# Four cross-attention layers on one core: the softmax of the narrow layers read straight from PSUM

## The reference

```
narrow (layers 0, 3):  xn = x / sqrt(mean(x^2) + 1e-5) * norm_w
                       q = xn Wq (16 heads of 8);  k, v = ctx Wk, ctx Wv (4 heads of 8, each for 4 query heads)
                       x = x + softmax(q k^T / sqrt(8)) v Wo
wide (layers 1, 2):    q = x Wq; k, v = ctx Wk, ctx Wv (16 heads of 64)
                       x = x + softmax(q k^T / 8 + col_bias) v Wo + bo
```

## Time and profile before

| | |
|---|---|
| median of 3 runs | 418.3 us (417.02 to 418.61) |
| profiled execution, its own time | 416.49 us |
| its span | 414.7 us |
| mean granted clock of TensorE | 0.978 |
| share of the span busy: PE, DVE, ACT, POOL | 91%, 68%, 64%, 47% |
| exponentials (L432) | 512 of 389 ns |
| narrow, wide maxima (L545) | 256 of 343 ns, 256 of 283 ns |

### The profile page before, as it was taken

One profiled execution on the slowest core, in us unless ns is written; L12 is line 12 of the kernel. 1 busy time (PEld: TensorE's weight loads), 2 busy tenths in 40 slices (PEclk: granted clock), 3 DMA queues, 4 the chain that ended last, 5 costly groups with the idle time before them and its releaser, 6 DMA issues.

```text
span 414.7 us, 10513 instructions
## 1 busy us (share of the span) xinstructions
PE 377.7 (91%) x3536; PEld 326.8 (79%) x3536; DVE 279.9 (68%) x1439; ACT 265.7 (64%) x1143; POOL 194.4 (47%) x222
## 2 busy tenths in 40 slices
PE   5686989999999999988997999999999999987865
PEld 4565877898899998877875878889999988866644
DVE  5578468564647656578475777758775575688993
ACT  4456567775657565567474777769865765666680
POOL 5845534332324233466472776424433333667751
PEclk9696989999999999999999999999999999999999
DMA  8705100000000000000000000000000000000000
GB/s 267 303 3 213 42 0 3 2 2 0 4 0 2 2 2 2 1 2 2 2 7 9 8 3 6 2 2 2 2 2 2 2 2 1 2 2 2 8 9 13
DMA packets 4740, 9.72 MB, mean 23 GB/s; under 512 B 592, under 2 KB 3152, under 8 KB 4432
## 3 DMA queue, kind: packets, MB, share of 16 engines
q1 hardware_dynamic: 4400, 8.72, 5.7%
q10 hardware_dynamic: 288, 0.33, 0.3%
HBM read 8.53 MB, written 0.52 MB: 22 GB/s over the span
## 4 chain that ended last, share of the span: by engine, by line
PE 75%; DVE 17%; ACT 3%; issue 2%; DMA 1%; POOL 1%; ACTq 0%; DVEq 0%; POOLq 0%
PE pt_ps L757 12%; PE scores_ps L744 8%; DVE probs L545 8%; PE v_ps L806 8%; PE fill_ps L629 7%; PE q_ps L711 7%; PE fill_ps L630 7%; PE fill_ps L631 7%; PE v_ps L776 6%; PE v_ps L788 6%; PE scores_ps L731 5%; DVE probsT L556 4%; ACT probs L432 2%; DVE oT L563 1%; DMA tok_i<-in_tokens 1%
## 5 line engine op out<-in xcount | busy, mean ns | idle before, releaser
L432 ACT ACTIVATE probs<-probs,negmax 128x128 f32<-128x128 f32 x512 | 198.4, 389 | 120.1 <-DVE negmax L545 120.1
L342 POOL TENSOR_TENSOR probs<-probs,inv 128x512 f32<-128x512 f32 x128 | 133.1, 1040 | 204.5 <-DVE inv L552 203.1
L432 ACT ACTIVATION_READ_ACCUMULATOR probs<-probs,negmax 128x1 f32 x512 | 95.6, 187 | 0.0
L545 DVE CUSTOM_DVE_ANT_0 probs<-scores_ps,col_bias,inv_rms 128x128 f32<-128x128 f32 x256 | 73.4, 343 | 22.7 <-PE scores_ps L731 22.3
L556 DVE COPY probsT<-pt_ps 128x512 f32<-128x512 f32 x128 | 82.1, 682 | 4.2 <-PE pt_ps L757 2.1
L545 DVE CUSTOM_DVE_ANT_0 probs<-scores_ps,col_bias 128x128 f32<-128x128 f32 x256 | 58.2, 283 | 37.8 <-PE scores_ps L744 37.8
L757 PE MATMUL pt_ps<-smalls,probs 128*128 128x128 f32 x512 | 71.7, 284 | 0.0
L757 PEld LDWEIGHTS pt_ps<-smalls,probs 128*128 128x128 f32 x512 | 56.3, 144 | 12.2 <-issue 10.9
L629 PE MATMUL fill_ps<-c_hi,w_hi 128*128 128x256 f32 x128 | 39.1, 305 | 4.6 <-DVE kn_lo L516 4.6
L545 DVE DVE_READ_ACCUMULATOR2_ANT negmax<- 128x1 f32 x512 | 42.4, 83 | 0.0
L776 PE MATMUL v_ps<-probsT,v_narrow 128*32 128x128 f32 x512 | 35.0, 280 | 6.9 <-issue 3.3
(11 more groups left out here) (87 smaller groups left out, 567.5 us busy)
## 6 DMA issues: line engine op xcount, KB each, us to landing
kT<-in_kv_w SPq DMA_DIRECT2D x6, 512.0 KB, 6.7
w_qo<-in_qo_w SPq DMA_DIRECT2D x2, 1024.0 KB, 9.6
v<-in_ctxT SPq DMA_DIRECT2D x4, 256.0 KB, 3.9
v<-in_kv_w SPq DMA_DIRECT2D x2, 512.0 KB, 11.1
outT<-x SPq DMA_DIRECT2D x8, 64.0 KB, 1.6
x<-in_xT SPq DMA_DIRECT2D x1, 384.0 KB, 7.9
oT<-in_narrow_kv ACTq DMA_DIRECT2D x1, 320.0 KB, 3.0
wn<-in_narrow_w SPq DMA_DIRECT2D x2, 128.0 KB, 4.8
```

Source lines behind the costliest of these rows:

```text
L342: nc.gpsimd.tensor_tensor(p4, p4, inv[:, o % 2, side, :].unsqueeze(2).broadcast_to([P, 4, S]), ALU.mult,).then_inc(probs_made[side], 1)
L432: last = nc.scalar.activation(e, e, ACT.Exp, scale=-1.0, bias=negmax[:, o % 2, side, q:q + 1], accum_out=rowsum[:, o % 2, side, q:q + 1])
L545: last = nc.vector.tensor_tensor_reduce(out=probs[:, o % PROBS_RING, side, cols], in0=scores_ps[side][:, cols], in1=bias, scale=scale, sca ...
```

## The change

In narrow octets, each side's four custom instructions give way to one tensor_reduce (maximum over keys, 512 columns of PSUM into 4) and a tensor_scalar that multiplies these four by inv_rms and -1. A semaphore most_made stands between the two. The exponentials of narrow octets read the scores in PSUM, with inv_rms as the scale and negmax as the bias, and write probs. The queries are no longer negated. The wait for rms_made moves from ahead of the scores' wait to behind the first reduction. The scores of the next octet wait, where the octet before in the same bank was narrow, for exps_made of both sides instead of scores_read. Octets from LAST_FILL + 2 = 55 on that are odd count as using the fill_ps banks: narrow ones (57, 59, 61, 63) write there. Octet 55 is wide and still writes scores_ps, and waits for the fill banks' reads. The third plane of col_bias and its memset go.

```diff
@@ exponentials
+                n = o // 2
                 act.wait_ge(scores_read[side], o + 1)
                 for q in range(4):
-                    e = probs[:, o % PROBS_RING, side, q * S:(q + 1) * S]
-                    last = nc.scalar.activation(e, e, ACT.Exp, scale=-1.0, bias=negmax[:, o % 2, side, q:q + 1],
+                    cols = slice(q * S, (q + 1) * S)
+                    e = probs[:, o % PROBS_RING, side, cols]
+                    if is_narrow(n):
+                        scores, scale = banks[scores_bank(o)][side][:, cols], inv_rms[:, n % 2:n % 2 + 1]
+                    else:
+                        scores, scale = e, -1.0
+                    last = nc.scalar.activation(e, scores, ACT.Exp, scale=scale, bias=negmax[:, o % 2, side, q:q + 1],
                                                 accum_out=rowsum[:, o % 2, side, q:q + 1])
@@ scores_out
-                if l in NARROW and h == 0 and side == 0:
-                    dve.wait_ge(rms_made, narrow_index(n) + 1)
                 dve.wait_ge(scores_full[side], o + 1)
+                if l in NARROW:
+                    use = 2 * narrow_index(n) + h + 1
+                    nc.vector.tensor_reduce(most[:, side, :], banks[scores_bank(o)][side][:].rearrange("p (h k) -> p h k", h=4),
+                                            mybir.AxisListType.X, ALU.max).then_inc(most_made[side], 1)
+                    if h == 0 and side == 0:
+                        dve.wait_ge(rms_made, narrow_index(n) + 1)
+                    dve.wait_ge(most_made[side], use)
+                    nc.vector.tensor_scalar(negmax[:, o % 2, side, :], most[:, side, :], inv_rms[:, n % 2:n % 2 + 1], -1.0,
+                                            ALU.mult, ALU.mult).then_inc(scores_read[side], 1)
+                    return
@@ scores (TensorE)
-                if o > 0:
-                    pe.wait_ge(scores_read[0], o)
-                    pe.wait_ge(scores_read[1], o)
+                out, m = banks[scores_bank(o)], previous_scores(o)
+                if m is None and o > 0:
+                    for i in range(2):
+                        pe.wait_ge(fill_read[i], len(FILL_ORDER[i::2]))
+                if m is not None:
+                    for side in range(2):
+                        pe.wait_ge(exps_made[side] if is_narrow(m // 2) else scores_read[side], m + 1)
@@ new functions
+LAST_FILL = max(FILLS)
+def scores_bank(o):
+    return "fill" if o >= LAST_FILL + 2 and o % 2 == 1 else "scores"
+def previous_scores(o):
+    return next((m for m in range(o - 1, -1, -1) if scores_bank(m) == scores_bank(o)), None)
```

More of the change, by code:

```diff
@@ L148, in build @@
         v_ps, q_ps = bank("v_ps"), bank("q_ps")
+        banks = {"scores": scores_ps, "fill": fill_ps}
         y_ps, qn_ps, ms_ps = v_ps[:, 0:T], q_ps[:, 0:T], q_ps[:, T:2 * T]
@@ L167, in build @@
         suppress = sb("suppress", [P, 2])
-        col_bias = sb("col_bias", [P, 3, S])
+        col_bias = sb("col_bias", [P, 2, S])
         mean_w = sb("mean_w", [P, P])
@@ L192, in build @@
         probsT = sb("probsT", [P, 2, BANK])
+        most = sb("most", [P, 2, 4])
         negmax = sb("negmax", [P, 2, 2, 4])
@@ L231, in build @@
         scores_full, scores_read = pair("scores_full"), pair("scores_read")
+        most_made = pair("most_made")
         exps_made, inv_made, probs_made = pair("exps_made"), pair("inv_made"), pair("probs_made")
@@ L525, in narrow_queries @@
                                         ).then_inc(rms_out, 1)
-                nc.vector.tensor_scalar(qn_hi[:, n % 2], qn_ps, -NARROW_SCALE, None, ALU.mult).then_inc(qn_hi_made, 1)
+                nc.vector.tensor_scalar(qn_hi[:, n % 2], qn_ps, NARROW_SCALE, None, ALU.mult).then_inc(qn_hi_made, 1)
                 dve.wait_ge(qn_hi_made, use)
                 nc.vector.scalar_tensor_tensor(
-                    out=qn_lo[:, n % 2], in0=qn_ps, scalar=-NARROW_SCALE, in1=qn_hi[:, n % 2].bitcast(F32),
+                    out=qn_lo[:, n % 2], in0=qn_ps, scalar=NARROW_SCALE, in1=qn_hi[:, n % 2].bitcast(F32),
                     op0=ALU.mult, op1=ALU.subtract).then_inc(qn_lo_made, 1)
@@ L537, in scores_out @@
                 l, b = job(n)
-                bias = col_bias[:, 2 if l in NARROW else l - 1, :]
-                scale = inv_rms[:, n % 2:n % 2 + 1] if l in NARROW else 1.0
-                if l in NARROW and h == 0 and side == 0:
-                    dve.wait_ge(rms_made, narrow_index(n) + 1)
                 dve.wait_ge(scores_full[side], o + 1)
+                if l in NARROW:
[8 more added lines that the diff above has]
+                    return
+                bias = col_bias[:, l - 1, :]
                 for q in range(4):
@@ L545, in scores_out @@
                     last = nc.vector.tensor_tensor_reduce(
-                        out=probs[:, o % PROBS_RING, side, cols], in0=scores_ps[side][:, cols], in1=bias, scale=scale,
+                        out=probs[:, o % PROBS_RING, side, cols], in0=scores_ps[side][:, cols], in1=bias, scale=1.0,
                         scalar=HUGE, op0=ALU.add, op1=ALU.min, accum_out=negmax[:, o % 2, side, q:q + 1])
@@ L604, in half @@
                     split_piece(o)
-            nc.vector.memset(col_bias[:, 2, :], 0.0)
             dve.wait_ge(keys_made, 1)
@@ L730, in scores @@
                             rows = slice(32 * (2 * h + side), 32 * (2 * h + side) + 32)
-                            last = nc.tensor.matmul(scores_ps[side][:], queries_part[rows, n % 2, :],
+                            last = nc.tensor.matmul(out[side][:], queries_part[rows, n % 2, :],
                                                     keys_part[rows, :], start=(m == 0), stop=(m == 2))
```

## The result

The changed kernel takes 427.7 us, the median of 4 runs (427.06 to 428.05), against 418.5 us for the kernel before in the same session: ratio 1.021, 95% interval 1.016 to 1.027. The forecast was 422.0 with a range to 426.0. Run again unedited beside 17 runs of the kernel before, the change stands at 1.015 (1.008 to 1.023), 427.2 us. So it is slower by 1.5 to 2%, 6.4 to 9.3 us, where the forecast had 3.7. All ratios leave out runs more than 1.5% above the quickest of their kernel, so they can differ a little from the ratio of the medians.

The account below looks back on a forecast made before the run. It took TensorE as the bound in octets 24 to 39 and VectorE in the last narrow octets. Middle +3.5, start +1.8 and late -1.6 gave +3.7 on the median 418.3: 422.0 us, range 414.5 to 426.0.

Parts of the forecast that it names:

- Given back: After octet 3's later scores: longer idling displaces work at the lower clock, returning 1.0 us of the +2.8.
- Start: First narrow octets: octet 3's scores come 2.8 us later, less 1.0 returned through the clock; +1.8 us.
- Exponentials: Narrow octets on ScalarE: 457 ns each, midway between 407 and 507, +68 ns; +0.54 us for an octet's eight.
- Maxima: Narrow octets on VectorE: reduction 682 ns plus product and wait, 0.94 us; each side 0.27 us shorter, 0.54 an octet.
- Its reader on GpSimd is idle then ... so I cost this at nothing: Side 1's inverse of sums, behind the next octet's first maximum: its delay costs nothing; without cover 1 us an octet.
- Middle: Octets 24 to 39: scores waiting for exponentials, less shorter kn_lo waits, plus a ScalarE copy wait; +3.5 us.
- Five waits of 0.86: Middle octets: scores start 0.86 us later in five short intervals, held for exponentials; +4.3 us.
- Two kn_lo waits: Middle, at 196.19 and near 224 us: shorter maxima bring kn_lo earlier, giving back 2 x 0.54 us.
- Late: Last narrow octets: shorter maxima release qn_lo and even scores earlier, three times 0.54 us; -1.6 us in sum.
- (c): Rival, narrow octets: exponential takes 507 ns, +0.67 us an octet; 428.2 us, chance 0.13.
- (a): Rival, narrow octets: operand cheap, exponential takes 407 ns, sum 0; 418.3 us, chance 0.27.
- (b): Rival, narrow octets: second operand costs nothing, exponential takes 339 ns, kernel gets faster; 414.0 us, chance 0.15.

Follow-up runs that it names:

- e3_swap: Changed kernel with the reciprocal of the previous octet's side 1 sums moved behind both sides' maxima; 425.0 us, ratio 1.011.
- e11_start_only: Kernel before, with the new form and the moved reciprocal in octets 0 to 7 alone; 426.1 us, ratio 1.015.
- e7_late_only: Kernel before up to octet 55; new form, second banks and moved reciprocal in octets 56 to 63 alone; 419.5 us, ratio 0.998.
- e5_hold3: Kernel before, with only octet 3's scores held until octet 2's exponentials are done; 425.7 us, ratio 1.012.
- e13_banks_only: Kernel before, with only the second banks for scores of late odd octets, old form everywhere; 422.1 us, ratio 1.006.
- e4_warm: Changed kernel with 22 matmuls on constant tiles, results unused, before octet 3's scores; 427.7 us, ratio 1.018.

## Why the prediction was wrong

The sign and most terms came out, but the sum was too small. The step that failed first is "Given back" in **Start**: the lower level of the clock was to end when it did before, or to last as long, and it lasted half as long again.

- **Exponentials.** 457 taken, 462 measured: right, and so is the choice between the ends. The operand costs 83 ns, within the 68 to 118 of the rows. What eight of them add to an octet was put at 0.54 us and is 0.44: 3.64 us from the first's start at 247.32 to the last read's end at 250.96, against 3.20. They overlap, and from one start to the next are 0.44 us instead of 0.39, so the pitch grows by 0.05 where the instruction itself grows by 0.07.
- **Maxima.** The reduction at 672 ns (682 taken) and the product at 0.23 us where it runs free are right; the first exponential starts 1.10 us after the scores' end instead of 1.36. Side 1's product was mis-sized: 0.53. "Its reader on GpSimd is idle then ... so I cost this at nothing" saw the queues and not that the reader, once released, holds up VectorE's next short instruction. In the middle, where side 0 sets the start of the exponentials, it only lengthens what VectorE reaches behind it, and it matters late.
- **Middle.** Five waits of 0.86 were forecast, and the intervals of octets 28, 32, 34 and 36 are 0.81 to 0.82 longer, that of 25 0.69. Two kn_lo waits (0.95 and 2.60 us idle before) were to save 1.1, and in the changed kernel save 0.5 (0.98 and 2.05). With the swap they save the 1.1 (0.67 and 1.74), so the blocked product took the rest. With 0.2 more for a ScalarE copy that is 3.9 - 0.5 + 0.2 = 3.6 us, against the +3.5. The trace shows +5.0, because octet 26's interval took 10.8 us at a low clock (9.4 before, 8.9 in e3_swap); no row of before could show that. That 3.6 met +3.5 is in part luck: the waits came out 0.4 us too long and the saving 0.6 too large.
- **Start, the step that failed.** "scores of 3 start at 38.84 instead of 36.01: +2.8" has the right mechanism: 2.7 us more between the scores of octets 2 and 3, 2.9 in e11_start_only. Yet they stand at 39.93, 3.9 later than before, though octet 0's are 0.9 earlier. The two octets ahead took 16.4 us, against 14.2 in the profile of before and 16.0 in e7_late_only with the old form, so most of this surplus is the quick profile of before. "Given back ... I take 1.0" failed. Its mechanism exists: in e5_hold3, where the lower level lasted 6.9 us as before, 0.9 of 2.1 us came back. In the changed kernel the lower level lasted from 36.2 to 46.5 us, 10.3 instead of the 6.9 before (34.9 to 41.8), and nothing came back: from octet 3's scores to octet 4's are 9.97 us, against 9.60 before. The four profiles with 6.1 to 6.4 us of idle time before octet 3's scores (the change twice, e3, e11) have 10.2 to 10.3 us at the lower level there, the seven with 3.5 to 5.6 us have 6.8 or 6.9. Of the two cases that the forecast named, a return at the same time and one as long after the restart, the second is near: from the restart to the return are 6.6 us, against 5.8 before.
- **Start, the other terms.** The new form, with the swap, also costs 1.1 us in octet 0 and 0.9 in octets 5 and 7 (e11_start_only against e7_late_only), which the forecast had at 0.27 and at nothing; that the dearer exponentials are the cause there is not shown. +1.8 was forecast; 4.4 is measured against e7_late_only's start, 6.2 against the profile of before. By the ratios the change's whole loss can be had with the start alone (1.015), by the medians and at equal clock some two thirds of it.
- **Late.** -1.6 forecast, +1.0 measured. With the reciprocal moved it is -1.2 (e3_swap, one profile at full clock; four others with the swap take 49.0 to 50.1 at a lower one), so the mechanism is borne out. The changed kernel lost it to the product of 0.45 to 0.53 us on three of four sides, and 1.2 us more to one interval at low clock (7.4 us instead of 6.2 behind octet 56). The gaps before even scores were to be 1.1, 0.5 and 0.3 us and are 1.49, 0.92 and 0.73. The second banks alone bring nothing (e13_banks_only); they are needed because of the hold, as the forecast had it.
- **Baseline.** The forecast scaled by a median of 3 runs, 418.3. The median of 79 others is 420.8; of the distance from 422.0 to 427.7, some 2 us may be that.
- **The rivals.** (c) came nearest in time, 428.2, but by an exponential of 507 ns that does not exist. (a) and (b) fall with the 462.

What stays open: what sets the granted clock at a place, and so why the lower level lasted longer. In e4_warm it did not follow the filled wait, but had lasted longer ahead of it, and the extra work overran the wait. The profiles of e5_hold3 and e11_start_only have it lower in code that these edits left alone, and so have others at other places; a link is not shown. And how the start's loss divides between octet 3's wait and the rest: the traces give 2.9 of 4.8 us to it, the medians about 1, the runs at equal clock about 2, and none of these is clear of the others.

## What to carry to other kernels

Before an instruction is made to read its input straight from a PSUM bank, work out how long the bank is then held and who queues behind it; a copy that looks wasteful may be what frees the bank early. Two edits that each save work can meet in one queue: what a moved instruction releases on a neighbouring engine counts as part of its cost. And where the same kernel spreads over 2% with its granted clock, give what the clock may return both signs in the forecast, and compare stretches of two traces only where their clock agrees. A mean clock over a long stretch can hide that two stretches in it went opposite ways.

## What the runs showed of the hardware

- A second per-partition operand on ScalarE's exponential of 128 columns costs 83 ns (462 against 379), and reading PSUM instead of SBUF saves 10 (379 against 389). The accumulator read that follows takes 217 ns behind a PSUM source with one operand, 207 with two, 187 to 189 behind an SBUF source.
- A VectorE product of 4 columns in SBUF took 0.23 us alone. When it started beside GpSimd's tensor_tensor it took up to 0.53 us in the change and once 1.28 in e3_swap. All 37 long ones of the change ended 23 to 27 ns after an instruction of GpSimd.
- GpSimd's power took 0.61 us for one column and 20.7 for 128.
- One kernel's runs spread over 9 us (415.8 to 424.8), 2.4 us for each hundredth of mean granted clock.
- A wait of 2.1 us in a stretch at the lower level of the clock (36.8 to 43.7 us in e5_hold3) cost 1.2 us there, since it displaced work at half speed. Where TensorE had stood idle for 6.1 to 6.4 us at this place, that stretch lasted 10.2 to 10.3 us instead of 6.8 or 6.9.
